# Five output images of a fused wavelet convolution, batch norm and median kernel: the mix of an image is added in DRAM by transfers of the POOL queue, and image 15 gets its mix in a bank of its own

## What is computed

```python
    x = _L0_conv_ref(x, ...)          # wavelet images, 3x3 convolution, then:
    #   y = conv + convW_b ;  x = relu(y * scale + shift)   (batch norm over all 16 images)
    x_denoised = median_blur(x, 3)    # median of 3x3 neighbours, zero padded
    y = jnp.einsum('bchw,oc->bohw', x_denoised, W) + b[None, :, None, None]
    return x + y
```

## Time and profile before

| | us |
|---|---|
| median of 3 runs | 402.18 |
| lowest, highest | 400.51, 403.07 |
| the profiled execution | 403.58 |
| its span (first to last instruction or transfer) | 401.2 |
| PE busy in the span | 383.8 |
| DVE busy in the span | 372.2 |
| POOL busy in the span | 232.5 |
| ACT busy in the span | 170.8 |

### The profile page before, as it was taken

The page is one execution under the profiler, slowest core; times in us unless marked ns, Lnnn a source line. Parts: engine busy times, 40 slices in busy tenths (PEclk is TensorE's granted clock), DMA queues, the critical chain, the costliest instruction groups (busy, mean ns, idle before and its releaser), DMA issues.

```text
span 401.2 us, 3603 instructions
## 1 busy us (share of the span) xinstructions
PE 383.8 (96%) x1106; PEld 205.1 (51%) x1106; DVE 372.2 (93%) x487; ACT 170.8 (43%) x351; POOL 232.5 (58%) x213
## 2 busy tenths in 40 slices
PE   6889999999999999999999999999999999998776
PEld 2245578866454555555555545454545464443222
DVE  2889967999999999999999999999999999999994
ACT  2456674446252433333334343333424221379661
POOL 3999559460694664738474747465564740016791
PEclk9999999999999999999999999999999999999988
DMA  7980010010101001010101010101011000002665
GB/s 290 418 364 2 2 52 2 0 52 2 53 1 52 17 37 52 0 52 0 54 0 52 1 54 1 52 1 52 8 46 33 19 2 1 0 0 119 247 248 223
DMA packets 7793, 26.69 MB, mean 67 GB/s; under 512 B 992, under 2 KB 1248, under 8 KB 7776
## 3 DMA queue, kind: packets, MB, share of 16 engines
q1 hardware_dynamic: 7776, 26.48, 17.6%
HBM read 18.09 MB, written 8.39 MB: 66 GB/s over the span
## 4 chain that ended last, share of the span: by engine, by line
PE 81%; DVE 12%; POOL 3%; DMA 2%; issue 1%; SPq 0%; ACT 0%; DVEq 0%
PE conv_ps L429 60%; PE conv_ps L444 12%; PE one_ps L411 4%; PE one_ps L530 3%; DVE y L1004 2%; PE conv_ps L554 2%; DMA z<-x 2%; POOL y L241 1%; POOL y L242 1%; DVE one_ps L916 1%; DVE one_ps L925 1%; DVE sorted_cols L876 1%; DVE sorted_cols L923 1%; DVE one_ps L910 1%; DVE sorted_cols L883 1%
## 5 line engine op out<-in xcount | busy, mean ns | idle before, releaser
L429 PE MATMUL conv_ps<-ru,wt 128*128 128x512 f32 (+1 forms) x324 | 129.9, 537 | 0.0
L429 PEld LDWEIGHTS conv_ps<-ru,wt 128*128 128x128 f32 x324 | 61.3, 190 | 55.1 <-issue 52.7
L429 PE MATMUL conv_ps<-xu,wt 128*128 128x496 f32 (+3 forms) x216 | 86.6, 537 | 0.0
L663 ACT ACTIVATE y<-conv_ps,sgn 128x512 f32<-128x512 f32 (+1 forms) x36 | 24.4, 679 | 124.1 <-PE conv_ps L429 124.1
L429 PEld LDWEIGHTS conv_ps<-xu,wt 128*128 128x128 f32 x216 | 41.0, 190 | 35.6 <-issue 33.7
L248 POOL TENSOR_TENSOR ru<-z 128x512 f32<-128x512 f32 x14 | 18.2, 1301 | 59.3 <-DVE one_ps L916 59.3
L342 POOL TENSOR_TENSOR ru<-eo 128x512 f32<-128x512 f32 x16 | 17.0, 1062 | 47.5 <-DVE one_ps L874 47.4
L429 PE MATMUL conv_ps<-ru,v 128*128 128x496 f32 (+3 forms) x108 | 43.3, 537 | 0.0
L554 PE MATMUL conv_ps<-z,w 128*128 128x512 f32 x64 | 32.7, 653 | 7.4 <-POOL z L387 4.1
L411 PE MATMUL one_ps<-y,w 128*128 128x512 f32 x64 | 30.5, 601 | 5.1 <-POOL y L242 1.8
L620 ACT ACTIVATE z<-z,bn 128x256 f32<-128x256 f32 x64 | 33.1, 595 | 0.4 <-DVE bn L819 0.4
(11 more groups left out here) (141 smaller groups left out, 741.1 us busy)
## 6 DMA issues: line engine op xcount, KB each, us to landing
z<-x SPq DMA_DIRECT2D x16, 512.0 KB, 10.5
raw_place<-x SPq DMA_DIRECT2D x15, 512.0 KB, 3.2
out<-y SPq DMA_DIRECT2D x15, 512.0 KB, 2.6
wt<-w_t SPq DMA_DIRECT2D x2, 576.0 KB, 10.8
ru<-x SPq DMA_DIRECT2D x1, 512.0 KB, 14.1
out<-y SPq DMA_DIRECT2D x2, 256.0 KB, 2.6
w<-w_t SPq DMA_DIRECT2D x2, 64.0 KB, 7.9
vec<-vectors SPq DMA_DIRECT2D x1, 3.0 KB, 8.3
```

The source lines that it names most:

```text
L429: return nc.tensor.matmul(bank(u, b)[:, (r0 - row) * BW:(r1 - row) * BW], taps(half, kx, ky), plane[:, (r0 + dy) * BW:(r1 + dy) * BW], sta ...
L663: S.activation(at(slot(n), row * W + b, [[2, cols]]), src, ACT.Identity, scale=sgn[:, :], accum_out=y_sum[:, part:part + 1]).then_inc(y_ke ...
```

## The change

`SUMMED` becomes 1, 3, 6, 8, 10. For these images x1 is now computed by POOL with the same kind of instruction as the other maps, as `max(scale*y, -shift)`, and what it lacks (+ shift) is added by ACT with the b when it takes the mix from PSUM. SP sends this x1 to DRAM early. When it has landed, POOL issues a transfer that adds the mix to it in DRAM (`accum_op`). ACT's L720 and POOL's L393 and L398 are gone. The mix of image 15 goes to `one_ps`, where the medians had their scratch rows, so PE does not wait for `finish(13)` before it. The eight interleaved finishes stand one median step later, and the batch norm computes one more column.

```diff
-    SUMMED = (1, 3, 7, 9, 12)
+    SUMMED = (1, 3, 6, 8, 10)
-    BN3_AT, FINISH_AT = 11, (15, 17, 19, 21, 23, 25, 27, 29)
+    BN3_AT, FINISH_AT = 11, (16, 18, 20, 22, 24, 26, 28, 30)
...
-            for n in range(IMAGES - 1):
-                if n in SUMMED:
-                    sp.wait_ge(out_by_pool, SUMMED.index(n) + 1)
-                else:
-                    sp.wait_ge(out_ready, OWN.index(n) + 1)
+            ahead = list(SUMMED)
+            for n in OWN[:-1]:
+
+                while ahead and ahead[0] < n + 3:
+                    m = ahead.pop(0)
+                    sp.wait_ge(x1_by_pool, m + 1)
+                    sp.dma_start(out_img[:, m, :], slot(m)).then_inc(x1_sent[m], 16)
+                sp.wait_ge(out_ready, OWN.index(n) + 1)
                 sp.dma_start(out_img[:, n, :], slot(n)).then_inc(out_sent, 16)
...
-            sp.wait_ge(out_sent, 16 * (IMAGES + 1))
+            sp.wait_ge(out_sent, 16 * (len(OWN) + 1))
+            for n in SUMMED:
+                sp.wait_ge(mix_sent[n], 16)
...
+            def add_mix(n):
+
+                pool.wait_ge(mix_kept, SUMMED.index(n) + 1)
+                pool.wait_ge(x1_sent[n], 16)
+                G.dma_start(out_img[:, n, :], zslot(n), accum_op=ALU.add).then_inc(mix_sent[n], 16)
+
             def map_x1(n):
-                G.tensor_scalar(slot(n), slot(n), scale3[:, :], shift3_bias2[:, :], ALU.mult, ALU.add).then_inc(x1_by_pool, 1)
+
+                if n in SUMMED:
+                    G.tensor_scalar(slot(n), slot(n), scale3[:, :], neg_shift3[:, :], ALU.mult, ALU.max).then_inc(x1_by_pool, 1)
+                else:
+                    G.tensor_scalar(slot(n), slot(n), scale3[:, :], shift3_bias2[:, :], ALU.mult, ALU.add).then_inc(x1_by_pool, 1)
...
-                if n in OWN:
-                    map_x1(n)
+                map_x1(n)
                 if n - 3 in SUMMED:
-                    pool.wait_ge(x1_by_act, SUMMED.index(n - 3) + 1)
-                    pool.wait_ge(mix_kept, SUMMED.index(n - 3) + 1)
-                    G.tensor_tensor(slot(n - 3), slot(n - 3), zslot(n - 3), ALU.add).then_inc(out_by_pool, 1)
+                    add_mix(n - 3)
...
+            def mixed(n):
+
+                return one_ps[:, 0, :] if n == IMAGES - 1 else conv_ps[:, n % 2, :]
...
-            for n in range(2, IMAGES):
+            for n in range(2, IMAGES - 1):
...
-                mix(n, n % 2)
+                mix(n)
+            mix(IMAGES - 1)
...
-                if n in SUMMED:
-                    S.activation(slot(n), slot(n), ACT.Relu, bias=shift3[:, :], scale=scale3[:, :]).then_inc(x1_by_act, 1)
                 if n - 2 in SUMMED:
                     act.wait_ge(mix_done, n - 1)
-                    S.activation(zslot(n - 2), conv_ps[:, n % 2, :], ACT.Identity, bias=cb2).then_inc(mix_kept, 1)
+                    S.activation(zslot(n - 2), conv_ps[:, n % 2, :], ACT.Identity, bias=shift3_bias2[:, :]).then_inc(mix_kept, 1)
...
+                after(1)
+                step(V.scalar_tensor_tensor(neg_shift3[:, :], mid3[:, :], scale3[:, :], b3, ALU.mult, ALU.subtract))
```

More of the change, by code:

```diff
@@ L124, in wavelet_conv_median_kernel @@
         zero_cols = at(zeros[:, :], 0, [[0, BANK // CH], [1, CH]])
-        singles = sb("singles", [CH, 19])
+        singles = sb("singles", [CH, 20])
         (abs_g3, neg_abs_g3, signed_b, beta_bias2, y_total, sq_total, mean3, off3, neg_off3, sq_eps3, var3, sd3, r3, newton3,
-         scale3, neg_scale3, shift3, shift3_bias2, mid3) = (singles[:, k:k + 1] for k in range(19))
+         scale3, neg_scale3, shift3, shift3_bias2, mid3, neg_shift3) = (singles[:, k:k + 1] for k in range(20))
         conv_ps = ctx.enter_context(nc.psum_tensor("conv_ps", [CH, 2, PIX], fp32))
@@ L189, in wavelet_conv_median_kernel @@
         med_normed = sem("med_normed")
-        x1_by_act = sem("x1_by_act")
         x1_by_pool = sem("x1_by_pool")
@@ L195, in wavelet_conv_median_kernel @@
         mix_kept = sem("mix_kept")
-        out_by_pool = sem("out_by_pool")
+        x1_sent, mix_sent = ({n: sem(f"{name}{n}") for n in SUMMED} for name in ("x1_sent", "mix_sent"))
         out_ready = sem("out_ready")
@@ L545, in _, with mix @@
             outputs(len(UNITS) - 1)
-            def mix(n, k):
+            def mixed(n):
+                return one_ps[:, 0, :] if n == IMAGES - 1 else conv_ps[:, n % 2, :]
+            def mix(n):
                 if 0 < n < IMAGES - 1:
@@ L553, in mix @@
                     half = slice(b * BANK, (b + 1) * BANK)
-                    mm = nc.tensor.matmul(conv_ps[:, k, half], w2[:, :], zslot(n)[:, half], start=True, stop=True)
+                    mm = nc.tensor.matmul(mixed(n)[:, half], w2[:, :], zslot(n)[:, half], start=True, stop=True)
                     if b == 1 or n == IMAGES - 1:
@@ L564, in _ @@
             for n in range(2):
-                mix(n, n)
-            for n in range(2, IMAGES):
+                mix(n)
+            for n in range(2, IMAGES - 1):
                 if n - 2 in SUMMED:
@@ L997, in second_batch_norm @@
                 step(V.scalar_tensor_tensor(shift3[:, :], mid3[:, :], neg_scale3[:, :], b3, ALU.mult, ALU.add))
+                after(1)
+                step(V.scalar_tensor_tensor(neg_shift3[:, :], mid3[:, :], scale3[:, :], b3, ALU.mult, ALU.subtract))
                 V.scalar_tensor_tensor(shift3_bias2[:, :], mid3[:, :], neg_scale3[:, :], beta_bias2[:, :], ALU.mult, ALU.add).then_inc(bn3_ready, 1)
             def finish(n, first=0, count=PIX, part=0):
-                dve.wait_ge(x1_by_pool, OWN.index(n) + 1)
+                dve.wait_ge(x1_by_pool, n + 1)
                 dve.wait_ge(mix_done, n + 1 + part)
                 v = slot(n)[:, first:first + count]
-                V.scalar_tensor_tensor(v, v, cb2, conv_ps[:, n % 2, first:first + count], ALU.max, ALU.add).then_inc(out_ready, 1)
+                V.scalar_tensor_tensor(v, v, cb2, (one_ps[:, 0, :] if n == IMAGES - 1 else conv_ps[:, n % 2, :])[:, first:first + count], ALU.max, ALU.add).then_inc(out_ready, 1)
             place = {BN3_AT: second_batch_norm}
```

## The result

| | kernel before | changed kernel |
|---|---|---|
| median, us | 401.64 (6 runs) | 407.01 (6 runs) |
| lowest, highest | 400.51, 403.07 | 406.0, 407.7 |
| ratio, 95% interval | | 1.0133 [1.0108, 1.0158] |
| span of the profiled execution | 401.2 | 404.9 |
| end of the last median instruction (E) | 391.83 | 395.50 |

The forecast was 401.2 us with a range of 397.6 to 403.9. The time lies outside it, on the slow side. Of the 3.7 us in the spans, E is 3.7 later, and behind E nothing was gained where 2.7 had been expected. The changed kernel is up to 0.1 us earlier where the tail begins (355.45 against 355.56 in the earlier trace rows), so all of it arises in the tail.

A forecast was written before the change was run, and what follows sets the result against it. DVE was taken to set the pace up to 391.83 us, then a chain through all engines. Terms of +1.7 up to E and -2.7 behind it gave -1.0 in all: 401.2 us, range 397.6 to 403.9.

The forecast's parts named there:

- +1.7 up to E: Tail up to the last median instruction's end: -3.03 - 0.37 + 0.13 + 3.1 + 1.9 us.
- POOL's maps grow from 11 to 16, at 1.19 us each: POOL in the tail: 16 maps fill 19 of about 36 us, each able to delay DVE by up to 1.2.
- The adding transfers are hidden: End of the tail: last adding transfer issued some 11 us ahead; 2.6 to 10 us hidden, 14.1 would add 3.1.
- rival D: End moves to POOL's queue, the last adding transfer landing after everything else: slower, 404.3 if landing takes 14.1 us; chance 0.08.
- E + 6.7: End of the span: last finish ends at E + 3.7, then 3.0 us; before, the end was E + 9.4.
- DVE's meetings with maps, +3.1: Tail: POOL's maps hold up two-tile DVE instructions at four meetings, +3.1 us in sum, bounds 1.3 and 4.8.
- The idle stretch of PE and the clock: Before mix(2): PE idle 3.3 us, then 1.2 GHz clock for 6.8 us; DVE waits about 0.6 + 1.3 = 1.9.
- POOL issues five transfers, 1.0 us each: POOL's queue in the tail: each issue taken as 1.0 us, between 0.33 and 2.37; same end for 0, 0.33 and 1.0.
- The sums' waits leave DVE, -3.03: DVE in the tail: waits of 0.97 and 1.74 us under sums and 0.32 under map(6) go, together -3.03 us.
- the last finish ends at E + 3.7: After E: the second half of mix(15) is done at E + 2.8, and the last finish ends at E + 3.7.
- The -2.7 behind E: From E to the span's end: E + 6.7 instead of E + 9.4, partly because the low clock had made mixes late.

The follow-up runs named there:

- the last two runs: Changed kernel with x1 by ACT and early finishes, only images 1, 3, 6 (then only 1, 3) added in DRAM, others summed by POOL: 399.72 and 399.76 us.
- the run of forms: Changed kernel with another form of POOL's map for each of the five SUMMED images; one execution, no total time given.
- the run with both edits: Changed kernel with POOL's five maps as mult and add instead of mult and max, and transfers without adding: 400.68 us, ratio 0.9964.

## Why the prediction was wrong, step by step

The sum had +1.7 up to E and -2.7 behind it. Measured are +3.7 and 0.0, so the two parts missed by 2.0 and 2.7 us.

- **POOL's maps grow from 11 to 16, at 1.19 us each: failed.** The row of 1.19 is one of mult and add. The new five are mult and max: 4.2 us by the rows, 3.7 where they meet nothing. The step took a duration from a row of the same instruction name, engine and shape and didn't ask whether the operation is the same. It cost about 3 us (1.0133 against 1.0058, and the last finish 3.8 earlier without it), by way of memsets, and thus mixes, that came late: DVE waited 4.3 us for PE where 1.9 had been forecast.
- **The adding transfers are hidden: failed as well.** It cost about 4 us (1.0133 against 1.0037); which of the two failures is the larger, the intervals leave open. The sum asked when the last one would land and found 11 us of room. That is true: the last one is issued at 391.3, and no transfer to `out` took more than 8.8 us to land, so what landed last at 404.9 was the second half of image 15, a plain transfer, which rival D did not have. What was missing is the load: five transfers of 3.1 us on engines that 16 images also need. The end of E + 6.7 became E + 9.4, of which E + 3.9 for the last finish was forecast well (3.7).
- **DVE's meetings with maps, +3.1: right in kind, a little high.** With fast maps they came to 2.4, and L883 lasted 1.26. In the changed kernel they come to 2.6, most of it (1.9) at L924. L883 lasted 0.69 there: the slow map of image 1 had been running for 2.9 us when it started (358.45 and 361.37), and so late in a slow map DVE is not held up (below).
- **The idle stretch of PE and the clock: happened, mis-sized.** 2.77 us idle, clock 0.50 over 364 to 366. It made finish(2) wait 0.74 (0.6 forecast) and finish(4) not at all (1.3 forecast). The forecast took the length of the fall, 6.8 us, from the one in the kernel before; here it lasted from about 363 to 366.5. The waits of 2.24 and 1.30 that did come have POOL's memsets behind them, the first with another fall of the clock.
- **POOL issues five transfers, 1.0 us each: right** (1.05 in the median row; 0.58 without adding). Only the bounds 0.33 and 2.37 had rows behind them, so the hit is luck, and little hung on it.
- **The sums' waits leave DVE, -3.03, and the last finish ends at E + 3.7: right** (E + 3.9).
- **The -2.7 behind E: mis-sized.** It was counted from an execution with the low clock late in the tail, and put on a median. About half of the executions of the kernel before have no such fall and are 2 us shorter; against them the new bank alone gained nothing (median spans 399.0 and 398.85). The forecast named the low clock as part of this gain; it was most of it. With the two costs away 0.7 us of span remain (398.1 against 398.8), and 1.2 in the last two runs.
- **The rivals:** D named the right part, an adding transfer, but by its own landing, and gave it 0.08. None of them had POOL as the bound through its own maps.

## What to carry to other kernels

An instruction's price belongs to its operation, not only to its name, engine and shape: before a cost is copied from a row, the operations have to be the same. A transfer that is off the critical path still takes DMA time from those on it, so cost it twice: when it lands, and what it adds to the busy share of the engines in the stretch where the last outputs go. If work is moved from one engine to another to relieve the first, add up the second one's queue with the new durations before looking at any wait. And before a gain is worked out from one profile, compare its granted clock with that of the other executions: here the baseline's profile held 2 us that half of its executions do not have.

## What the runs showed of the hardware that was not expected

- POOL's TENSOR_SCALAR on 128x1024 fp32 takes 1.20 us as mult and add. From start to next start it takes 3.2 us as max alone, 3.65 as mult and max with a constant, and 3.73 to 3.74 as mult and max with a column, mult and min, max and mult, mult and subtract.
- A slow form holds up DVE instructions with two SBUF inputs only early in its run. Those that start 0.6 us behind its start take 1.14 to 1.26 us instead of 0.69 (L916 at 371.64 beside the map of 371.03 to 374.94, the same in the run without adding and in the run of forms), which is what one takes at the same place beside a fast map (1.14 for L916 in the run with both edits). Where DVE was ahead, the map waits instead: the one of 382.30, beside L924 and L926, lasts 4.95. Those that start 1.6 us or more behind it take 0.69 to 0.73 (L918 at 372.81, L883 at 361.37), although the row goes on. Beside a sum the wait lasts to the sum's end (2.43 for L916 in the earlier trace rows). The Trainium skill ("SBUF — State Buffer", "Who interferes with whom") has a GpSimd instruction that reads SBUF hold the port for the whole instruction; for the fast forms and the sums the traces agree, for the slow form they do not.
- An adding transfer of 512 KB to DRAM takes 2.8 to 3.2 us of all 16 DMA engines, by the run, a plain one from the same queue 1.3.
- Behind the issue of an adding transfer the ends of POOL's rows move, but not their starts. In the changed kernel the issue at 374.76 lasts 1.05 us, the memset 0.58 and the map 1.65, and the next row starts at 376.59; in the run without adding the same rows last 0.58, 0.12 and 1.20 from 374.73, and the next starts at 376.55. What waits for such an end still comes late: mix(7) starts at 376.08 against 375.58.
- An idle stretch of PE of 1.9 us near 386 was followed by the low clock in the kernel before but not in the run with only mix(15) moved, where the stretch is the same. In the changed kernel one of 2.30 us was followed by it and one of 2.25 was not. Stretches of 2.8 to 3.3 us were followed by it in every profile that has them here. The low clock lasted 6.8 us in the kernel before and about 3.4 each time in the changed one.
